# A vision tower's attention and merged-weight network on one core: engine orders up to the gates changed, merging products from 18 to 32 rows

## What is computed

```python
# tokenizer: shifted copies of the image, 16x16 patches as one product
y = conv(xs, conv_w) + conv_b
h = layernorm(y) * gamma + beta
h = h @ dense_w + dense_b
# attention: 8 heads of 16, two softmaxes, the second subtracted
attn = softmax(q1 k1 / 4) - lam * softmax(q2 k2 / 4)
o = attn @ v
xn = groupnorm(o, 4 groups of 32 features, over features and tokens of an image) * gn_w + gn_b
h = layernorm(h + xn @ out_w.T + out_b)
# feed-forward: gates from the mean over the tokens of an image mix 8 expert weights into the base
g   = (relu(x @ gfc1_w.T + gfc1_b) @ gfc2_w.T + gfc2_b).mean(tokens)        # 8 per image
W1m = W1 + sum_e g[e] * tv_W1[e]       # 512 x 128 per image, W2m likewise
h1  = relu(x @ W1m.T + b1m)
out = h1 @ W2m.T + b2m
res = layernorm(x + out) * lng + lnb ; h = layernorm(h + res)
```

## Time and profile before

| | us |
|---|---|
| median of 3 runs | 219.09 |
| lowest, highest | 218.19, 219.74 |
| profiled execution | 218.36 |
| its span, first to last instruction | 216.5 |
| TensorE products busy | 178.9 (83%) |
| VectorE busy | 133.1 (62%) |
| ScalarE busy | 120.6 (56%) |
| GpSimd busy | 48.7 (22%) |

### The profile page before, as it was taken

How to read it: one execution, slowest core, us unless ns; L and a number is a source line. 1 busy time by engine, 2 the same in 40 slices (tenths; PEclk the granted TensorE clock), 3 DMA queues, 4 the chain that set the end, 5 groups by cost and what they waited for, 6 DMA issues and landing times.

```text
span 216.5 us, 7809 instructions
## 1 busy us (share of the span) xinstructions
PE 178.9 (83%) x3428; PEld 124.1 (57%) x3428; DVE 133.1 (62%) x247; ACT 120.6 (56%) x223; POOL 48.7 (22%) x76
## 2 busy tenths in 40 slices
PE   0888999999897999979999999999999999990000
PEld 0332445475586646635887888888878778770000
DVE  2593155468999699845664566666655544488750
ACT  2122365488793244679444577777764433346992
POOL 2001201675378156000000000000053000027740
PEclk9999999999999999999965999999999999998555
DMA  6999996222000000000021021313000000000112
GB/s 214 369 394 387 374 287 123 74 74 82 6 5 3 8 0 3 6 0 0 3 74 38 20 82 36 82 30 89 12 6 3 3 3 3 3 3 0 38 42 72
DMA packets 9265, 16.51 MB, mean 76 GB/s; under 512 B 1598, under 2 KB 4350, under 8 KB 8720
## 3 DMA queue, kind: packets, MB, share of 16 engines
q1 hardware_dynamic: 9232, 16.02, 23.6%
HBM read 15.20 MB, written 0.82 MB: 74 GB/s over the span
## 4 chain that ended last, share of the span: by engine, by line
PE 59%; DVE 14%; ACT 14%; SPq 4%; DMA 4%; issue 3%; ACTq 0%; DVEq 0%
PE PS L1378 16%; DVE arena L381 8%; PE PS L1400 8%; PE PS L1074 8%; PE PS L1124 5%; ACT t L765 4%; PE PS L1390 4%; DMA arena<-windows 4%; PE PS L1183 3%; PE PS L1241 3%; PE PS L1168 2%; ACT arena L592 2%; SPq L402 2%; ACT hid L592 2%; SPq L397 2%
## 5 line engine op out<-in xcount | busy, mean ns | idle before, releaser
L381 DVE COPY arena<-PS 128x1024 f32<-128x1024 f32 x32 | 39.0, 1224 | 36.5 <-PE PS L1378 36.5
L380 ACT ACTIVATE arena<-PS 128x1024 f32<-128x1024 f32 x32 | 32.7, 1024 | 23.3 <-PE PS L1378 23.2
L1378 PE MATMUL PS<-gates,wrow 18*128 18x128 f32 x1024 | 39.0, 292 | 1.7 <-DVE arena L381 0.7
L1378 PEld LDWEIGHTS PS<-gates,wrow 18*128 18x128 f32 x1024 | 33.0, 194 | 8.2 <-DVE arena L381 5.2
L1074 PE MATMUL PS<-arena,hid 128*128 128x512 f32 (+1 forms) x64 | 27.3, 554 | 8.2 <-ACT hid L556 6.2
L1074 PEld LDWEIGHTS PS<-arena,hid 128*128 128x128 f32 x64 | 11.2, 200 | 22.1 <-issue 13.5
L535 POOL TENSOR_TENSOR t<-t,lnaff 128x2048 f32<-128x2048 f32 x1 | 4.6, 4556 | 74.3 <-PE PS L1390 74.3
L1400 PE MATMUL PS<-arena,t 128*32 128x128 f32 x512 | 19.0, 294 | 0.0
L1424 PE MATMUL PS<-arena,hid 128*32 128x128 f32 x512 | 17.3, 276 | 0.0
L1400 PEld LDWEIGHTS PS<-arena,t 128*32 128x32 f32 x512 | 14.1, 117 | 2.2 <-issue 0.2
L765 ACT ACTIVATE t<-t,nms,rsl 128x128 f32<-128x128 f32 x32 | 13.4, 480 | 2.4 <-DVE nms L1044 2.4
(11 more groups left out here) (132 smaller groups left out, 296.2 us busy)
## 6 DMA issues: line engine op xcount, KB each, us to landing
arena<-windows SPq DMA_DIRECT2D x24, 256.0 KB, 8.0
wrow<-ffn_weights SPq DMA_DIRECT2D x32, 128.0 KB
hid<-conv_filter SPq DMA_DIRECT2D x8, 320.0 KB, 6.3
wrow<-ffn_weights SPq DMA_DIRECT2D x64, 8.0 KB
cst<-consts SPq DMA_DIRECT2D x1, 840.0 KB, 11.2
out<-t SPq DMA_DIRECT2D x16, 50.0 KB
cst<-consts SPq DMA_DIRECT2D x1, 322.0 KB, 9.0
arena<-windows SPq DMA_DIRECT2D x4, 64.0 KB, 8.7
```

Of the source, the lines that this page charges most:

```text
L380: return eng.activation(dst, PS[:, b:b + 2, :], ACT.Copy)
L381: return eng.tensor_copy(dst, PS[:, b:b + 2, :])
L1378: mm = pe.matmul(PS[:, merge_bank(n) + r, :].rearrange("p (b k j) -> p k b j", k=4, j=NJ)[:, k], wrow[32 * r:32 * r + KR, w], gates[32 * r ...
```

## The change

The orders of ScalarE, VectorE and TensorE are rewritten up to the gates. In TensorE's, `scores(6)` and `scores(7)` now stand ahead of `values(0)`, `small_products()` and the filler `keep_long(2, 7)` ahead of `scores(5)`, and there are ten `keep_long` products for eight. `x2_turn` waits for its own quarter. The gate product takes 32 columns of the constants from G0 on (18 of them the gate weights and zeros as before, the rest whatever follows in `cst`), and `rowc` is zero in the rows 18 to 31 of each group, so that `gates` is zero there. `wrow` is zeroed on GpSimd ahead of the first loads, which wait for it chunk by chunk, and the merging products take 32 rows.

```diff
@@ -443,6 +444,7 @@
               sp.dma_start(dst, base).then_inc(wrow_loaded[c], 16)
 
   for c in range(NC):
+      sp.wait_ge(wrow_zeroed, c + 1)
       load_rows(0, c)
   for c in range(NC):
       sp.wait_ge(merge_done, NQ * (c + 1))
...
@@ -487,6 +489,8 @@
   pool.wait_ge(headmask_ready, 2)
   for w, name in enumerate(("k1_b", "k2_b")):
       pool.tensor_tensor(kb[:, 4 * w:4 * w + 4], headmask[:, :], C(name).to_broadcast([P, 4]), ALU.mult).then_inc(kb_ready, 1)
+  for c in range(NC):
+      pool.memset(wrow[:, c * WSLOT:(c + 1) * WSLOT], 0.0).then_inc(wrow_zeroed, 1)
   pool.wait_ge(cst_loaded, 16)
   pool.tensor_scalar(cmat[:, :], ident, -1.0 / D, None, ALU.add).then_inc(cmat_ready, 1)
 
...
@@ -654,8 +658,8 @@
   h_evac(0)
   y_square(1)
   query_evac(0)
+  y_rstd(1)
   keys_evac(0, 1)
-  y_rstd(1)
   lambda_exp()
   h_evac(1)
   soft_exp(0)
...
@@ -664,16 +668,16 @@
   y_rstd(2)
   keys_evac(1, 1)
   h_evac(2)
+  y_square(3)
   soft_exp(1)
-  y_square(3)
+  y_rstd(3)
   keys_evac(2, 0)
-  y_rstd(3)
+  h_evac(3)
   keys_evac(2, 1)
-  h_evac(3)
   soft_exp(2)
+  keys_evac(3, 0)
   soft_exp(3)
   keys_evac(3, 1)
-  keys_evac(3, 0)
   soft_exp(4)
   v_evac(0)
   v_evac(1)
...
@@ -681,35 +685,35 @@
   v_evac(2)
   v_evac(3)
   o_part(0)
+  soft_exp(6)
   o_part(1)
-  soft_exp(6)
+  soft_exp(7)
+  group_square(0)
   o_part(2)
   o_part(3)
-  soft_exp(7)
-  group_square(0)
   group_rstd(0)
-  group_square(1)
   o_part(4)
   o_part(5)
   r_square(0)
-  group_rstd(1)
-  group_square(2)
   r_rstd(0)
+  group_square(1)
   o_part(6)
   o_part(7)
+  group_rstd(1)
+  x2_evac(0)
+  group_square(2)
+  group_square(3)
+  r_square(1)
   group_rstd(2)
-  r_square(1)
-  group_square(3)
-  x2_evac(0)
+  group_rstd(3)
+  gate_relu(0)
   r_rstd(1)
-  group_rstd(3)
   r_square(2)
-  gate_relu(0)
   r_square(3)
   r_rstd(2)
   r_rstd(3)
+  x2_evac(1)
   gate_relu(1)
-  x2_evac(1)
   gate_relu(2)
   gate_relu(3)
   x2_evac(2)
...
@@ -928,59 +932,59 @@
   soft_sum(0)
   lambda_minus()
   key_raw()
+  y_scale(2)
   query_evac(1, 1)
-  y_scale(2)
   soft_shift(1)
+  query_evac(0, 2)
   soft_sum(1)
-  query_evac(0, 2)
-  soft_shift(2)
   y_scale(3)
   query_evac(1, 2)
+  soft_shift(2)
+  small_evac()
   prob_transpose(0)
   soft_shift(3)
   query_evac(0, 3)
   soft_sum(2)
+  soft_shift(4)
   soft_sum(3)
   query_evac(1, 3)
-  soft_shift(4)
-  small_evac()
   soft_shift(5)
   soft_sum(4)
-  prob_transpose(1)
   soft_sum(5)
   soft_shift(6)
+  soft_shift(7)
   o_sum(0)
   o_sum(1)
-  soft_shift(7)
   group_sum(0)
+  prob_transpose(1)
+  group_centre(0)
+  soft_sum(6)
+  prob_transpose(2)
+  group_square_sum(0)
   o_sum(2)
-  soft_sum(6)
-  group_centre(0)
+  soft_sum(7)
   o_sum(3)
+  group_scale(0)
+  o_sum(4)
   group_sum(1)
-  group_square_sum(0)
-  prob_transpose(2)
-  soft_sum(7)
-  group_centre(1)
-  group_scale(0)
-  group_square_sum(1)
-  o_sum(4)
   o_sum(5)
   group_sum(2)
   prob_transpose(3)
-  group_centre(2)
-  group_square_sum(2)
-  group_scale(1)
+  group_centre(1)
+  x2_scale(0)
+  group_square_sum(1)
   o_sum(6)
-  x2_scale(0)
   o_sum(7)
   group_sum(3)
+  group_centre(2)
+  group_scale(1)
+  group_centre(3)
+  group_square_sum(2)
+  group_square_sum(3)
   group_scale(2)
-  group_centre(3)
-  group_square_sum(3)
   group_scale(3)
+  gate_sum(0)
   x2_scale(1)
-  gate_sum(0)
   x2_scale(2)
   x2_scale(3)
   gate_sum(1)
...
@@ -1225,6 +1229,7 @@
   def x2_turn(q):
 
       pe.wait_ge(o_ready, 16)
+      pe.wait_ge(x2_ready, q + 1)
       if q >= 2:
           pe.wait_ge(x2t_ready, q - 1)
       for g in range(4):
...
@@ -1261,15 +1266,15 @@
   conv(1, 7)
   proj(0, 0)
   proj(0, 1)
+  y_var(1)
   proj(0, 2)
   proj(0, 3)
   conv(2, 0)
   conv(2, 1)
-  y_var(1)
+  conv(2, 2)
   scores(0)
-  conv(2, 2)
+  dense(1)
   conv(2, 3)
-  dense(1)
   conv(2, 4)
   conv(2, 5)
   conv(2, 6)
...
@@ -1280,83 +1285,87 @@
   proj(1, 2)
   proj(1, 3)
   scores(1)
+  dense(2)
   conv(3, 0)
-  dense(2)
   conv(3, 1)
   conv(3, 2)
   conv(3, 3)
   conv(3, 4)
   conv(3, 5)
   conv(3, 6)
+  conv(3, 7)
   proj(2, 0)
-  conv(3, 7)
+  y_var(3)
   proj(2, 1)
+  proj(2, 2)
   scores(2)
-  y_var(3)
-  proj(2, 2)
+  dense(3)
   proj(2, 3)
+  small_products()
   scores(3)
-  dense(3)
   proj(3, 0)
   proj(3, 1)
   proj(3, 2)
+  scores(4)
   proj(3, 3)
-  scores(4)
-  small_products()
+  pe.wait_ge(lnaff_ready, 1)
+  keep_long(2, 7)
   scores(5)
   v_proj(0)
   v_proj(1)
+  scores(6)
   v_proj(2)
+  pe.wait_ge(shifted, 6)
+  keep_long(1, 1)
   v_proj(3)
-  scores(6)
+  scores(7)
   values(0)
   values(1)
-  pe.wait_ge(shifted, 6)
-  keep_long(1, 1)
-  scores(7)
+  pe.wait_ge(shifted, 7)
+  keep_long(2, 3)
+  residual(0)
+  residual(1)
+  group_mean(0)
   residual(2)
-  keep_long(1, 3)
   values(2)
   values(3)
-  residual(0)
-  group_mean(0)
-  residual(1)
   keep_long(2, 3)
+  keep_long(1, 3)
   group_var(0)
+  values(4)
+  keep_long(1, 3)
+  values(5)
+  out_proj(0)
   group_mean(1)
-  keep_long(2, 3)
-  values(4)
-  values(5)
-  keep_long(1, 3)
-  out_proj(0)
-  group_var(1)
-  group_mean(2)
   r_var(0)
   pe.wait_ge(o_ready, 12)
   keep_long(1, 6)
   values(6)
   values(7)
+  group_mean(2)
+  group_var(1)
+  residual(3)
+  x2_turn(0)
+  group_mean(3)
+  gate_hidden(0)
+  out_proj(1)
   group_var(2)
-  out_proj(1)
-  residual(3)
-  group_mean(3)
-  x2_turn(0)
+  group_var(3)
+  r_var(1)
   out_proj(2)
-  r_var(1)
-  group_var(3)
-  gate_hidden(0)
   out_proj(3)
   r_var(2)
   r_var(3)
+  x2_turn(1)
   gate_hidden(1)
-  x2_turn(1)
   gate_hidden(2)
   gate_hidden(3)
   x2_turn(2)
   x2_turn(3)
   pe.wait_ge(ghsum_done, NQ)
+  gate_cols = cst[:, COL["gfc2"][0] + G0:COL["gfc2"][0] + G0 + 32]
   for r in range(NR):
-      mm = pe.matmul(PS[32 * r:32 * r + KR, 1, 0:NI], C("gfc2")[:, G0:G0 + KR], ghsum, start=True, stop=True)
+      mm = pe.matmul(PS[32 * r:32 * r + 32, 1, 0:NI], gate_cols, ghsum, start=True, stop=True)
   mm.then_inc(gfc2_done, 1)
   keep_clock(5, 2)
   pe.wait_ge(gates_ready, NJ)
...
@@ -1375,8 +1384,8 @@
       for k in range(4):
           w = slice((cc % NC) * WSLOT + (4 * q + k) * P, (cc % NC) * WSLOT + (4 * q + k + 1) * P)
           for r in range(NR):
-              mm = pe.matmul(PS[:, merge_bank(n) + r, :].rearrange("p (b k j) -> p k b j", k=4, j=NJ)[:, k], wrow[32 * r:32 * r + KR, w],
-                             gates[32 * r:32 * r + KR, :], start=True, stop=True)
+              mm = pe.matmul(PS[:, merge_bank(n) + r, :].rearrange("p (b k j) -> p k b j", k=4, j=NJ)[:, k], wrow[32 * r:32 * r + 32, w],
+                             gates[32 * r:32 * r + 32, :], start=True, stop=True)
       mm.then_inc(merge_done, 1)
 
   def hidden_transpose(i):
```

More of the change, by code:

```diff
@@ L237, in build @@
         rowc_zeroed = sem("rowc_zeroed")
+        wrow_zeroed = sem("wrow_zeroed")
         rows_loaded = sem("rows_loaded")
@@ L1244, in _ @@
             conv(1, 0)
+            conv(0, 1)
             conv(1, 1)
-            conv(0, 1)
             conv(0, 2)
```

## The result

| | us |
|---|---|
| kernel before, median of 4 runs | 218.64 (217.6 to 219.74) |
| changed kernel, median of 4 runs | 212.93 (212.44 to 213.37) |
| ratio | 0.9738, 95% interval 0.968 to 0.9796 |
| profiled execution after | 213.37, span 211.6 |

A forecast was written before the change was run, and what follows sets the result against it. It took TensorE to bound the first weight stage, 10.24 us of it at half clock, and a string of waits from VectorE's softmax to bound the gates; 219.09 less 2.5 (orders) and 4.5 (clock) gave 212.1 us, range 210.3 to 216.9.

The forecast's parts named there:

- The clock term: First weight stage: 32-row merging products keep TensorE at full clock from 109.12 to 119.36 us; -4.5 us, bounds 0 and -4.7.
- The rule on the other side: Merges: the gate follows how busy the engine is, so padding rows would change nothing and the clock term would be 0.
- The orders' term: Up to the gates: new issue orders save waiting, last gate_sum near 99.4 instead of 101.9; -2.5 us, bounds 0 and -3.4.
- where they delay anything ... its reader is behind on VectorE anyway: Ten fillers ahead of the gates: delays such as group_var(0) by about 0.9 us cost nothing, since the reader is late.
- the replay: Following the new orders up to the gates with the old profile's rounded durations; it moves 40 steps and gives 2.5 us.
- a last gate_sum later than 101: End of the stretch up to the gates: forecast near 99.4 us; a start after 101 would show the prediction wrong.
- The tail: From group_sum(3) to the last gate_sum: ScalarE has more left to do, 12.3 us where it took 11.4.
- The slow rival: Ahead of the gates: clock falls near 88 us, +4.7, merges start cold, 4.5 not won; 221.3 us, chance 0.07.
- The costs taken as nothing: 32-row weight loads, POOL's four memsets (7.3 to 8.6 us, hidden before cmat) and later weight row loads: cost 0.
- The total: Whole kernel: 219.09 - 7.0 = 212.1 us, chance 0.55 for its own range 210.3 to 214.0.

The follow-up runs named there:

- the old orders' second run: The kernel before with its old orders and only the 32-row products, zeroed rows and load waits, run again: twelve executions, 213.38 to 217.28 us.
- two variants: Changed kernel with gate and merging products back at 18 rows, median 216.2 us; changed kernel with one filler less ahead of group_var(0), median 212.25 us.
- the 18-row variant: The changed kernel with gate and merging products back at 18 rows, new orders and zeroing kept: ten executions, median 216.2 us.
- the variant without four fillers: The changed kernel without the four long fillers around group_var(0) and values(4): four executions, 213.79 to 213.90 us.

## Why the prediction was right, and where not

**The clock term, -4.5.** Right in mechanism and, in the profiled pair, in size: 4.3. Over all executions it is smaller. The bias products, for which no warm row existed, took 1.01 us, not 0.75. What the prediction had wrong here is that it took the fall as a fixed part of every execution of the kernel before ("all of them very likely had it"). It is a chance: 38 of 56 executions had a long cold time, and some had none and took 213.4. So the rows are worth 3.2 to 3.6 us of median. They also take away the spread: 8 us between the fastest and slowest execution before, 2 us after.

**The rule on the other side** (the Trainium skill, "TensorE: Matmul & The Clock Gate", Part 1: the gate follows how busy the engine is). Read with no rows in it, the rule does not fit: 18-row merges nearly without gaps still had a long cold time in 4 of 6 executions (by their mean clock), and 24 or 32 rows with gaps kept it through the merges in every profile. If busy is read as how much of the array works, nothing here speaks against it; no run tests that reading by itself.

**The orders' term, -2.5.** This is the step that failed. In the profiled pair it was 0.5; between the kernels with 32 rows 1.6 of median, and part of that is not waiting saved but fewer cold stretches ahead of the gates (3 of 16 executions above 20.5 us, against 8 of 16). Between the executions with little cold time, 213.65 against 212.8 (medians of 8 and 13), the waiting saved is 0.9. Two warm profiles with 32 rows that start alike (the old orders' second run and the changed kernel's) say the same: the last gate_sum at 102.01 and at 101.11. By the steps: shift(7) ended at 72.0 (71.3 forecast), sum(7) at 80.0 (79.6), fair so far; transpose(3) started at 84.25, not 82.9; group_sum(3) at 89.5, not 87.1. The sentence that failed is "where they delay anything ... its reader is behind on VectorE anyway". A filler of 0.86 us stands on the chain just ahead of the 0.59 us that the last maximum waited for `scores(7)`; whether the filler cost that isn't shown, for without any filler the wait was 0.70 us, though behind a cold stretch. The third filler ahead of group_var(0) was on the path (0.7 us of median), and it pushed group_scale(0) behind GpSimd's multiply, where it took 1.80 us; no duration in the replay allowed for that. The row that would have warned me was there: in the kernel before the same multiply had taken 1.96 us at 82.12 beside a group_scale. The prediction counted it as a slowed multiply and did not ask who would lose if the order of the two turned round. The rest was lost between transpose(3) and group_sum(3) (5.2 us, as before the change; 4.2 forecast). VectorE waited 0.98 us for o_part(7) there, and that for `values(7)`. Two things held that up in the trace: a filler ahead of `values(6)` ran until 85.95, 0.47 us after the transpose was done, though the forecast had these products going at once; and TensorE stood idle for 0.70 us inside `values(7)`, where the code has no wait (0.42 in another profile of the same kernel). What that gap is stays open. The prediction named a last gate_sum later than 101 as a sign that it is wrong; it started at 101.31.

**The tail.** Forecast 12.3 us from group_sum(3) to the last gate_sum, measured 11.85, so the tail did not eat the gain. (The terms listed for it, 9.8 + 2.2 + 0.5, add up to 12.5, not 12.3; by them the orders' term would be -2.3.)

**The slow rival** had the clock fall near 88 us, at a cost of 4.7 us and with the merges cold. The place was right: two variants fell there in their profiles (88.2 and 88.4 us), and three of the changed kernel's 16 executions have some cold time beyond the end's. The size was not: it cost 1.1 us at the last gate_sum, and the merges were warm. (The 78% that the prediction gives for 84 to 100 us is its row for 92.0 to 97.4 alone.)

**The costs taken as nothing** were nothing: 186 ns for a load of 32 rows as for one of 18, the memsets ahead of cmat (7.04 us, just below the 7.3 to 8.6 forecast), and 1.9 us of SP's wait for them.

**The total**, 212.1 against 212.93, owes part of its closeness to luck. In medians both terms were too large, the clock by 0.9 to 1.3 us and the orders by 0.5 to 0.9. Against that the starting point, a median of three executions, was 0.9 above the median of the 56 that ran later (219.09 against 218.2). From 218.2 the same terms would have given 211.2, 1.7 below the measured time.

## What to carry to other kernels

Where small-contraction products stand alone for some microseconds on TensorE, look at the granted clock behind them. If it falls, try filling the row groups up with zeroed rows: here the loads and products took no longer (186 and 282 ns either way), and no profile with 24 or 32 rows has a fall in the merges. Fillers are not free; put them where no reader waits, count them one by one, and judge them by the spread of executions rather than by one profile. When orders are moved, look at which two-input VectorE operations come to lie beside GpSimd's large ones: behind the multiply the scale took 1.80 us, ahead of it 0.63. And before one profile is set against another, compare the start of an operation that stands ahead of every change; here it differed by half a microsecond.

## What the runs showed of the hardware that I had not expected

- How many rows of a 32-row group the products use decided here whether the granted clock survived the merges. Merges of 18 rows, with little or no gap: 27 us or more at half clock in many executions (4 of 10, 4 of 6, 2 of 6, 38 of 56). 24 or 32 rows: in none of 6, and none of 16 + 16 + 7 + 6 (where the fillers, or all but one, stayed). The added rows hold zeros, and it works all the same; rows with data in them weren't tried. Where the cold time of an execution lay is seen in the profiled ones alone; for the others it rests on their mean clock.
- The same program has a clock history that differs between executions: for the kernel before 18 to 36 us at half clock, 213.4 to 221.6 us.
- What cold time ahead of the gates costs depends on where it lies. Counted from the first query copy, 6.6 us of it at 69 to 76 us delayed the last gate_sum by 2.9 us (32 rows, old orders, two profiles), about as much per microsecond as in the merges, where 10.2 us cost 4.3. Some 3 us at 88 to 92 in the 18-row variant delayed it by 1.1. The 9.6 us at 78 to 88 in the variant without four fillers were cheaper: group_sum(3) came about 1 us late, where prob_transpose(3) had been 0.8 us early.
- TensorE has idle gaps of 0.4 to 1.5 us inside runs of 128 small `values` products where the code has no wait, in the same places in several profiles. Their cause is open.
